# Attention plus a gated feed-forward block on one core: six of eight unrolled attention groups become a hardware loop, and four small VectorE instructions are written in plainer forms

## The chip, the cores and the metric

The kernel runs on one core of one Trainium2 chip. A core has five engines, each with a queue of its own: TensorE (PE; its weight loads are listed apart as PEld), VectorE (DVE), ScalarE (ACT), GpSimd (POOL) and SyncE (SP), which here only issues DMAs. "PEq", "DVEq" and so on are the queues' own instructions. Engines wait for each other by semaphores. The metric is the device time of one execution in microseconds (us). Before the change it is 1223.88 us, the median of 3 runs (1222.38 to 1224.13).

## The reference, cut to what matters

```python
# x: (2, 2048, 256), 16 heads of 16
xn = layernorm(x)
q, k, v = split(einsum('btd,ed->bte', xn, w_in), 3)        # per head
att = einsum('bhqd,bhkd->bhqk', q, k) / sqrt(16)
att = where(causal, att, 0.0)                              # masked scores are 0, not -inf
out = einsum('bhqk,bhkd->bhqd', softmax(att), v)
y_attn = einsum('btd,ed->bte', out, w_out)
x_prev = shift xn by one token
xr, xk = mu_r*xn + (1-mu_r)*x_prev, mu_k*xn + (1-mu_k)*x_prev
y_ffn = sigmoid(xr @ W_r.T) * (square(relu(xk @ W_k.T)) @ W_v.T)
return x + y_attn + y_ffn
```

Since a masked score is 0 and not minus infinity, keys behind the diagonal still take part, each with the weight exp(0 - max).

## The kernel before, in words

Stage 1 (`stage_tokens`) normalises the tokens in chunks of 512, computes q, k, v and the feed-forward part, and stores them in DRAM. q and k are each split into three bf16 parts. It already has a hardware loop over its first sequence, which runs once; all numbers in it are constants.

Stage 2 (`stage_attention`) works through eight groups, G = 2i + p: i runs over the two sequences and the two halves of the channels, p over two groups of four heads in each. p also says which of two sets of buffers the group uses. A group has four units u of 512 queries. Unit u has 4(u + 1) key tiles kt of 128 keys. For each key tile and each of 4 heads h:

- TensorE computes the scores (L1090) into a ring of 3 PSUM buffers, ScalarE takes the exponential (L972) into a ring of 16 SBUF buffers, and two tiles later TensorE multiplies with the values (L1104). On the diagonal GpSimd masks a 128x128 block first (L920); a `sem_inc` stands ahead of each mask (L918).
- Between them TensorE computes "pieces" of scores (L236) of a later unit or of the next group, of which VectorE takes the row maxima: L251 for a whole piece, L247 with a mask for one on the diagonal. Ahead of L247 stands a `sem_inc` (L246) that waits for the piece.
- Behind the last piece of a unit come six small VectorE instructions (`max_step`, k = 0 to 5), each on 128 partitions x 16 elements. They turn the maximum into a negative shift in three bf16 parts, which become three rows of the operand of L1090.

Once per unit TensorE adds the keys behind the diagonal (L1114), with diagonal weights that GpSimd makes with one product of 128x2048 (L887). ScalarE copies the sums out (L959), and VectorE divides them (L1007 to L1018). Once per group SyncE loads the next group's q, k (12 DMAs, L199 and L200) and v_sb (L219), after unit 0 has ended. GpSimd then adds up 15 tiles of v_sb one behind the other (L228), ahead of unit 2's masks, and TensorE and ScalarE make the suffix sums in unit 3. The last group also computes the output tiles (L1136).

What sets the order: each engine's instructions stand in its queue in the order of its `group` function, by the tables `SHIFT_AT`, `SV_AT`, `SLOT_PIECES`. The counts that the waits compare with grow from group to group, and are built from G, u and kt. Before the change G is a Python number everywhere, so every wait has a constant.

Of the kernel before, what the change touches and what calls it, by code (L numbers as in the profile page):

```python
# [7 lines left out]
ALU = mybir.AluOpType  # L8
# [4 lines left out]
B, T, C = 2, 2048, 256  # L13
# [3 lines left out]
CC = C // P  # L17
CH = 512
NCH = T // CH
SUB = CH // P  # L20
# [103 lines left out]
class Operands:  # L124
# [129 lines left out]
    def max_step(self, dve, k, u, n, reduced):  # L254


        by_head = [self.shift[:, u, :, part].rearrange("p s h -> p h s") for part in range(3)]
        if k == 0:
            dve.wait_ge(self.piece_reduced, reduced + MRING)
            dve.tensor_reduce(self.raw_max[:].rearrange("p h s -> p (h s)"), self.part_max[:, u % 2, :, 0:u + 1], AX_X,  # L260
                              ALU.max).then_inc(self.raw_ready, 1)
        if k == 1:
            dve.wait_ge(self.raw_ready, n + 1)
            dve.scalar_tensor_tensor(self.row_max[:, u], self.raw_max[:], 1.0, self.floor[:, :, u * SUB:(u + 1) * SUB],  # L264
                                     ALU.mult, ALU.max).then_inc(self.max_ready, 1)
        if k == 2:
            dve.wait_ge(self.max_ready, n + 1)
            dve.scalar_tensor_tensor(by_head[0], self.row_max[:, u], -1.0, self.floor[:, :, 0:SUB],
                                     ALU.mult, ALU.add).then_inc(self.hi_ready, 1)
        if k == 3:  # L270
            dve.wait_ge(self.hi_ready, n + 1)
            dve.scalar_tensor_tensor(self.shift_rest[:], self.row_max[:, u], -1.0, by_head[0], ALU.mult,
                                     ALU.subtract).then_inc(self.rest_ready, 1)
        if k == 4:
            dve.wait_ge(self.rest_ready, n + 1)
            dve.scalar_tensor_tensor(by_head[1], self.shift_rest[:], 1.0, self.floor[:, :, 0:SUB],
                                     ALU.mult, ALU.add).then_inc(self.mid_ready, 1)
        if k == 5:
            dve.wait_ge(self.mid_ready, n + 1)
            dve.scalar_tensor_tensor(by_head[2], self.shift_rest[:], 1.0, by_head[1], ALU.mult,  # L280
                                     ALU.subtract).then_inc(self.shift_ready, 1)

    def after_piece(self, dve, f, n0, base, close):

# [459 lines left out]
def stage_attention(nc, ops, ident, ident16, attn_t, ffn_d, w_out_sb, out):  # L744
# [7 lines left out]
    with ExitStack() as ctx:  # L752
# [56 lines left out]
        def unit_of(i, p, u):  # L809

            return (i * 2 + p) * NCH + u

        @block.sync
        def _(sp):
            def place_shift(p, u, n):

                sp.wait_ge(shift_t_ready, n + 1)
                for part in range(3):
                    sp.dma_start(q_op[ROWS + part:ROWS + part + 1, p, :, u * CH:(u + 1) * CH],
                                 shift_t[part * GH:(part + 1) * GH, u % 2]).then_inc(shift_loaded[u % 2], 16)  # L820

            def keep_normed(i, p, u):

                sp.wait_ge(normed_ready, unit_of(i, p, u) + 3)
                for h in range(GH):
                    row = (p * GH + h) * HD
                    sp.dma_start(attn_t[row:row + HD, i, u * CH:(u + 1) * CH],
                                 normed[h * HW:h * HW + HD, u % 2]).then_inc(normed_stored[u % 2], 16)

            def store_chunk(n):  # L830
                sp.wait_ge(total_ready, SUB * (n + 1))
                sp.dma_start(out_tiles[n], total[n % ORING]).then_inc(out_stored[n % ORING], 16)

            def group(i, p, first=False, last=False):
                if not first:
                    keep_normed(i - 1 + p, 1 - p, NCH - 1)
                place_shift(p, 2, unit_of(i, p, 2))
                if not last:

                    sp.wait_ge(out_ready, unit_of(i, p, 0) + 1)  # L840
                    ops.load_group(sp, i + p, 1 - p)
                keep_normed(i, p, 0)
                keep_normed(i, p, 1)
                place_shift(p, 3, unit_of(i, p, 3))
                if last:
                    store_chunk(0)
                keep_normed(i, p, 2)
                if not last:
                    place_shift(1 - p, 0, unit_of(i, p, NCH))
                    place_shift(1 - p, 1, unit_of(i, p, NCH + 1))  # L850
                if last:
                    for n in range(1, OUT_CHUNKS):
                        store_chunk(n)
                    keep_normed(i, p, NCH - 1)
                    for n in range(OUT_CHUNKS, B * NCH):
                        store_chunk(n)


            sp.sem_inc(probs_ready, SRING)
            sp.sem_inc(probs_used, USED)  # L860
            sp.sem_inc(out_ready, 1)
            sp.sem_inc(sums_ready, 1)
            sp.sem_inc(normed_ready, 2)
            for half in range(2):
                sp.sem_inc(normed_stored[half], STORES)
                sp.sem_inc(shift_loaded[half], SHIFTS)
            place_shift(0, 0, 0)
            place_shift(0, 1, 1)
            group(0, 0, first=True)
            for i in range(B * CC - 1):  # L870
                group(i, 1)
                group(i + 1, 0)
            group(B * CC - 1, 1, last=True)
            for s in normed_stored:
                sp.wait_ge(s, STORES * (1 + B * NG * NCH // 2))
            for s in out_stored:
                sp.wait_ge(s, 16 * (B * NCH // ORING))

        @block.gpsimd
        def _(pool):  # L880
# [16 lines left out]
            def group(i, p, first=False, last=False):  # L897
                G = i * 2 + p
                for u in range(NCH):
                    if u == 2 and not last:  # L900

                        pool.wait_ge(v_after_ready, G * 4 + 4)
                        ops.add_up_after(pool, 1 - p, G + 1, i + 1 + p)
                    if last and u == 1:
                        pool.wait_ge(out_ready, unit_of(i, p, 0) + 1)
                        for n in range(ORING):
                            load_chunk(n)
                    if last and u == NCH - 1:
                        for n in range(ORING, B * NCH - 1):
                            load_chunk(n)  # L910
                    if u == NCH - 1 and not last:
                        spread_weight(0, unit_of(i, p, NCH))
                    for kt in range(SUB * u, SUB * u + SUB):
                        for h in range(GH):

                            slot = (KT0[u] + kt) * GH + h
                            pool.wait_ge(probs_ready, G * SLOTS + slot + 1 + SRING)
                            pool.sem_inc(passed, 1)  # L918
                            blk = probs[:, slot % PRING, 0:P]
                            pool.affine_select(out=blk, in_=blk, compare_op=ALU.is_ge, fill=0.0, base=0,  # L920
                                               pattern=[[1, P]], channel_multiplier=-1).then_inc(probs_masked, 1)
                    if last and u == NCH - 1:
                        load_chunk(B * NCH - 1)
                    if u < NCH - 1:
                        spread_weight(u + 1, unit_of(i, p, u + 1))

            spread_weight(0, 0)
            group(0, 0, first=True)
            for i in range(B * CC - 1):
                group(i, 1)  # L930
                group(i + 1, 0)
            group(B * CC - 1, 1, last=True)
# [2 lines left out]
        def _(act):  # L935
# [53 lines left out]
            for u in range(2):  # L989
                weight(u, u)  # L990
            group(0, 0, first=True)
            for i in range(B * CC - 1):
                group(i, 1)
                group(i + 1, 0)
            group(B * CC - 1, 1, last=True)
# [2 lines left out]
        def _(dve):  # L998
# [49 lines left out]
                        add_tile(k)  # L1048

            group(0, 0, first=True)  # L1050
            for i in range(B * CC - 1):
                group(i, 1)
                group(i + 1, 0)
            group(B * CC - 1, 1, last=True)
# [2 lines left out]
        def _(pe):  # L1057
# [124 lines left out]
            for u in range(2):  # L1182
                turn_shift(u, u, 0)
            group(0, 0, first=True)
            for i in range(B * CC - 1):
                group(i, 1)
                group(i + 1, 0)
            group(B * CC - 1, 1, last=True)
# [28 lines left out]
```

## Time and profile before

| | |
|---|---|
| median of 3 runs | 1223.88 us (1222.38 to 1224.13) |
| the profiled execution | 1224.13 us, span 1222.3 us |
| PE busy | 1127.3 us (92%), 7168 matmuls |
| DVE busy | 949.4 us (78%) |
| ACT busy | 743.4 us (61%) |
| POOL busy | 347.7 us (28%) |
| stage 2 begins | about 242 us |
| groups 1 to 6 | 371 to 1094 us, 120 to 121 us each |

Busy time is the time in which an engine executes at least one instruction. The ends of matmuls are modelled and overlap, so TensorE's 92% is not TensorE at its peak. Register, branch, semaphore and DMA-issuing instructions are not counted as busy. The chain of waits is followed back from the last instruction, at each step to what released it; "issue" in it is time in which the engine waited for nothing that the profile shows.

### The profile page before, as it was taken

To read this page: it belongs to the slowest core of one execution; us is meant where nothing else is said; L and a number is where in the kernel's file an instruction comes from. 1 tells how busy PE (TensorE), PEld (TensorE's weight loads), DVE (VectorE), ACT (ScalarE), POOL (GpSimd) and SP (SyncE) were. 2 spreads that over 40 slices of the span, in tenths; PEclk is the share of its full clock that TensorE was granted. 3 is DMA by queue.
4 is the path that set the end of the run, shared out by engine and by line. 5 is a ranking of instruction groups with operands and counts; after the bars stand their busy time and mean duration, and the time that the engine had idled before them with its cause. 6 is when DMAs were issued, how large, how long until landed. Compare 5 with 4: busy or idle time off the path is not lost.

```text
span 1222.3 us, 21443 instructions
## 1 busy us (share of the span) xinstructions
PE 1127.3 (92%) x7168; PEld 459.4 (38%) x7168; DVE 949.4 (78%) x2433; ACT 743.4 (61%) x1553; POOL 347.7 (28%) x716
## 2 busy tenths in 40 slices
PE   5889888789999999999999999999999999999998
PEld 3656544343333333333333333333233332333345
DVE  5757888778689858986888788778968986899623
ACT  3544433166766666667667766766677666666773
POOL 2212113132423232334132323332332233224121
PEclk9999999889999989999999999999999999999999
DMA  4577732309001900180028002700360045002033
GB/s 129 164 185 172 213 109 91 104 3 144 9 2 23 130 6 2 24 129 6 2 32 122 6 1 39 114 6 2 53 100 6 1 60 94 6 1 79 6 108 108
DMA packets 62353, 79.22 MB, mean 65 GB/s; under 512 B 7075, under 2 KB 52515, under 8 KB 61219
## 3 DMA queue, kind: packets, MB, share of 16 engines
q1 hardware_dynamic: 61091, 73.66, 30.1%
q0 software_dynamic: 1152, 4.19, 1.2%
q8 instruction: 57, 0.93, 0.3%
q14 instruction: 53, 0.43, 0.1%
HBM read 43.78 MB, written 29.36 MB: 60 GB/s over the span
## 4 chain that ended last, share of the span: by engine, by line
PE 49%; DVE 12%; DMA 9%; issue 4%; SPq 2%; POOL 2%; ACT 1%; DVEq 0%; POOLq 0%
PE ps_o L1104 15%; PE ps_s L1090 14%; PE ps_m L236 13%; DMA v_sb<-vpad_d 9%; DVE part_max L251 5%; DVE ps_m L247 3%; PE ps_m L1136 2%; PE ps_o L1114 2%; POOL after L228 2%; DVE row_max L264 1%; PE ps_x L1081 1%; DVE part_max L247 1%; PE ps_x L1082 1%; DVE turned L1007 1%; SPq L200 1%
## 5 line engine op out<-in xcount | busy, mean ns | idle before, releaser
L972 ACT ACTIVATE probs<-ps_s 128x512 f32<-128x512 f32 (+3 forms) x1280 | 610.2, 534 | 290.0 <-PE ps_s L1090 285.1
L251 DVE TENSOR_REDUCE part_max<-ps_m 128x1 f32<-128x512 f32 x730 | 473.8, 680 | 33.7 <-PE ps_m L236 32.2
L1090 PE MATMUL ps_s<-q_op,k_op 99*128 99x512 bf16 (+3 forms) x1280 | 431.1, 355 | 8.8 <-ACT probs L972 6.0
L236 PE MATMUL ps_m<-k_op,q_op 96*128 96x512 bf16 (+3 forms) x1200 | 402.5, 355 | 33.5 <-DVE part_max L251 23.4
L247 DVE CUSTOM_DVE_ANT_0 ps_m<-ps_m,mask 128x384 f32<-128x384 f32 x470 | 229.2, 496 | 122.1 <-PE ps_m L236 120.4
L1104 PE MATMUL ps_o<-probs,v_sb 128*32 128x512 f32 (+3 forms) x2560 | 303.0, 546 | 4.8 <-POOL probs L920 4.8
L920 POOL TENSOR_SCALAR_AFFINE_SELECT probs<-probs 128x128 f32<-128x128 f32 x512 | 143.2, 296 | 396.3 <-ACT probs L972 389.6
L1090 PEld LDWEIGHTS ps_s<-q_op,k_op 99*128 99x128 bf16 x1280 | 122.0, 98 | 325.2 <-ACT probs L972 219.3
L236 PEld LDWEIGHTS ps_m<-k_op,q_op 96*128 96x128 bf16 x1200 | 117.9, 98 | 199.4 <-DVE part_max L251 92.6
L887 POOL TENSOR_TENSOR diag_weight<-ident,masked_weight 128x2048 f32<-128x2048 f32 x32 | 115.5, 3610 | 121.2 <-ACT masked_weight L939 121.2
L1104 PEld LDWEIGHTS ps_o<-probs,v_sb 128*32 128x32 f32 x2560 | 50.8, 108 | 94.0 <-issue 36.7
L228 POOL TENSOR_TENSOR after<-after,v_sb 128x64 f32<-128x64 f32 x120 | 40.0, 333 | 134.2 <-DMA v_sb<-vpad_d 125.4
L247 DVE DVE_READ_ACCUMULATOR2_ANT part_max<- 128x1 f32 x512 | 71.6, 140 | 0.0
L670 PE MATMUL ps_qk<-xn_t,w_in_sb 128*128 128x512 f32 x128 | 60.6, 609 | 1.7 <-ACT xn_t L597 1.4
L441 POOL TENSOR_TENSOR k_act<-k_act 128x1024 f32<-128x1024 f32 x8 | 15.4, 1919 | 126.5 <-ACT k_act L635 126.5
L602 ACT ACTIVATE parts<-ps_qk 128x512 bf16<-128x512 f32 x32 | 19.0, 594 | 46.7 <-PE ps_qk L670 46.7
L236 PE MATMUL ps_pieces<-k_op,q_op 96*128 96x512 bf16 (+2 forms) x80 | 25.6, 355 | 18.4 <-DVE part_max L251 9.2
L446 POOL TENSOR_TENSOR ffn<-ffn,x_in 128x512 f32<-128x512 f32 x16 | 21.5, 1342 | 57.8 <-DVE ffn L525 57.8
L607 ACT CAST parts<-rest 128x512 bf16<-128x512 f32 x32 | 19.7, 616 | 28.9 <-DVE rest L513 28.9
L1114 PE MATMUL ps_o<-diag_weight,v_after 128*32 128x128 f32 x1024 | 37.2, 291 | 0.0
L670 PEld LDWEIGHTS ps_qk<-xn_t,w_in_sb 128*128 128x128 f32 x128 | 24.4, 196 | 26.8 <-issue 22.5
L1136 PE MATMUL ps_m<-w_out_sb,attn_t 128*128 128x256 f32 x128 | 31.6, 381 | 0.5 <-DVE v_sb L1025 0.5
(84 smaller groups left out, 819.7 us busy)
## 6 DMA issues: line engine op xcount, KB each, us to landing
parts_d<-parts SPq DMA_DIRECT2D x48, 256.0 KB, 3.2
q_op<-parts_d SPq DMA_DIRECT2D x42, 256.0 KB, 13.1
k_op<-parts_d SPq DMA_DIRECT2D x42, 256.0 KB, 15.2
vpad_d<-v_pad SPq DMA_DIRECT2D x32, 256.0 KB, 3.5
v_sb<-vpad_d SPq DMA_DIRECT2D x8, 1024.0 KB, 26.8
x_in<-x SPq DMA_DIRECT2D x8, 512.0 KB, 5.4
ffn_d<-ffn SPq DMA_DIRECT2D x8, 512.0 KB, 3.2
attn_t<-normed SPq DMA_DIRECT2D x128, 32.0 KB, 2.0
```

The costliest lines, as they stand in the source:

```text
L228: pool.tensor_tensor(self.after[:, j], self.after[:, j + 1], values[:, j + 1, :, 0:HD], ALU.add).then_inc(self.after_ready, 1)
L236: last = pe.matmul(ps_m[:, f % ring, 0:width], self.q_op[0:ROWS, p, h, q0:q0 + P], self.k_op[0:ROWS, p, h, pc * CH:pc * CH + width], start ...
L247: dve.tensor_tensor_reduce(ps_m[:, f % ring, 0:width], ps_m[:, f % ring, 0:width], self.mask16[:, CH - width:CH], 1.0, LOWEST, ALU.add, AL ...
L251: dve.tensor_reduce(self.part_max[:, u % 2, h * SUB + s, pc:pc + 1], ps_m[:, f % ring, 0:width], AX_X, ALU.max).then_inc(self.piece_reduce ...
L670: last = pe.matmul(ps_qk[:, j % 2], w_in_sb[:, cc, j * P:(j + 1) * P], xn_t[:, cc, 1:CH + 1], start=(cc == 0), stop=(cc == CC - 1))
L887: pool.tensor_tensor(diag_weight[:, u % 2], ident[:].unsqueeze(1).broadcast_to([P, GH * SUB, P]), masked_weight[:, u].unsqueeze(2).broadca ...
L920: pool.affine_select(out=blk, in_=blk, compare_op=ALU.is_ge, fill=0.0, base=0, pattern=[[1, P]], channel_multiplier=-1).then_inc(probs_mas ...
L972: act.activation(probs[:, slot % PRING, 0:width], ps_s[:, slot % SRING, 0:width], ACT.Exp).then_inc(probs_ready, 1)
L1090: pe.matmul(ps_s[:, slot % SRING, 0:CH - q0], k_op[0:KROWS, p, h, kt * P:(kt + 1) * P], q_op[0:KROWS, p, h, u * CH + q0:(u + 1) * CH], sta ...
L1104: last = pe.matmul(ps_o[h * HW:(h + 1) * HW, q0:CH], v_sb[:, p, kt, h * HW:(h + 1) * HW], probs[:, ((KT0[u] + kt) * GH + h) % PRING, 0:CH ...
L1114: last = pe.matmul(ps_o[h * HW:(h + 1) * HW, s * P:(s + 1) * P], v_after[:, p, u * SUB + s, h * HW:(h + 1) * HW], diag_weight[:, u % 2, h ...
L1136: last = pe.matmul(ps_m[:, k % MRING, 0:C], attn_t[:, b * CC + cc, c * CH + t * P:c * CH + (t + 1) * P], w_out_sb[:, cc], start=(cc == 0), ...
```

## The change

In stage 2, the Python loop over groups 1 to 6 becomes `Fori`, a loop that each engine runs in its own queue: three rounds of two groups, `group(i, 1)` and `group(i + 1, 0)`. i is then a register. Group 0 and group 7 stay outside. The functions called are the same; a wait's number that depends on i is computed from the register before the wait, and so is the address of a DMA that depends on i. In `max_step`, four instructions that used a multiplication by one, or the zero constant `floor`, as a third operand are written without it.

```diff
         if k == 1:
             dve.wait_ge(self.raw_ready, n + 1)
-            dve.scalar_tensor_tensor(self.row_max[:, u], self.raw_max[:], 1.0, self.floor[:, :, u * SUB:(u + 1) * SUB],
-                                     ALU.mult, ALU.max).then_inc(self.max_ready, 1)
+            dve.tensor_tensor(self.row_max[:, u], self.raw_max[:], self.floor[:, :, u * SUB:(u + 1) * SUB],
+                              ALU.max).then_inc(self.max_ready, 1)
         if k == 2:
             dve.wait_ge(self.max_ready, n + 1)
-            dve.scalar_tensor_tensor(by_head[0], self.row_max[:, u], -1.0, self.floor[:, :, 0:SUB],
-                                     ALU.mult, ALU.add).then_inc(self.hi_ready, 1)
+            dve.tensor_scalar(by_head[0], self.row_max[:, u], -1.0, None, ALU.mult).then_inc(self.hi_ready, 1)
...
         if k == 4:
             dve.wait_ge(self.rest_ready, n + 1)
-            dve.scalar_tensor_tensor(by_head[1], self.shift_rest[:], 1.0, self.floor[:, :, 0:SUB],
-                                     ALU.mult, ALU.add).then_inc(self.mid_ready, 1)
+            dve.tensor_copy(by_head[1], self.shift_rest[:]).then_inc(self.mid_ready, 1)
         if k == 5:
             dve.wait_ge(self.mid_ready, n + 1)
-            dve.scalar_tensor_tensor(by_head[2], self.shift_rest[:], 1.0, by_head[1], ALU.mult,
-                                     ALU.subtract).then_inc(self.shift_ready, 1)
+            dve.tensor_tensor(by_head[2], self.shift_rest[:], by_head[1], ALU.subtract).then_inc(self.shift_ready, 1)
...
             place_shift(0, 0, 0)
             place_shift(0, 1, 1)
             group(0, 0, first=True)
-            for i in range(B * CC - 1):
+            with sp.Fori(0, B * CC - 1) as i:
                 group(i, 1)
                 group(i + 1, 0)
             group(B * CC - 1, 1, last=True)
... (the same for pool, act, dve and pe)
```

What stands in TensorE's queue, at the beginning of a unit 1: before,

```order
L1114 MATMUL ps_o<-diag_weight,v_after 32x128 [waits v_after_ready,diag_ready]
L1114 MATMUL ps_o<-diag_weight,v_after 32x128 x15
L1090 MATMUL ps_s<-q_op,k_op 128x512 [waits probs_ready]
L236 MATMUL ps_m<-k_op,q_op 128x256 [waits piece_reduced]
L1090 MATMUL ps_s<-q_op,k_op 128x512 [waits probs_ready]
L236 MATMUL ps_m<-k_op,q_op 128x512 [waits piece_reduced]
```

and in the loop (the lines of the new kernel are 3 lower; ISA is a register instruction):

```order
L1107 ISA
L1108 ISA [waits diag_ready]
L1111 MATMUL ps_o<-diag_weight,v_after 32x128 [waits v_after_ready]
L1111 MATMUL ps_o<-diag_weight,v_after 32x128 x15
L1086 ISA
L1087 MATMUL ps_s<-q_op,k_op 128x512 [waits probs_ready]
L234 ISA
L236 MATMUL ps_m<-k_op,q_op 128x256 [waits piece_reduced]
L1086 ISA
L1087 MATMUL ps_s<-q_op,k_op 128x512 [waits probs_ready]
L234 ISA
L236 MATMUL ps_m<-k_op,q_op 128x512 [waits piece_reduced]
```

The matmuls keep their order; ahead of each one that waits stands a register instruction. SyncE's queue, at the loads of the next group (the twelve loads alternate between q_op and k_op): before,

```order
L199 DMA q_op<-parts_d 16x4x2048 [waits out_ready]
L200 DMA k_op<-parts_d 16x4x2048
L199 DMA q_op<-parts_d 16x4x2048
L200 DMA k_op<-parts_d 16x4x2048
```

and in the loop:

```order
L837 ISA
L199 ISA [waits out_ready]
L199 DMA q_op<-parts_d 16x4x2048
L200 ISA
L200 DMA k_op<-parts_d 16x4x2048
L199 ISA
L199 DMA q_op<-parts_d 16x4x2048
L200 ISA
L200 DMA k_op<-parts_d 16x4x2048
```

Each load has a register instruction ahead of it, since its address depends on the round; one more stands ahead of v_sb (L219).

## Rows read from the trace of the kernel before

**Rows 1.** The page: span, and busy time, share and instructions of two engines.
```profile
span 1222.3 us, 21443 instructions
PE 1127.3 (92%) x7168; PEld 459.4 (38%) x7168; DVE 949.4 (78%) x2433; ACT 743.4 (61%) x1553; POOL 347.7 (28%) x716
```

**Rows 2.** Busy time of each engine in six stretches, groups 1 to 6.
```profile
core 0: us, PE busy (x) PEld busy (x) DVE busy (x) ACT busy (x) POOL busy (x), PEclk, DMA share, GB/s
371.00:491.00 120.00, 113.56 (x787) 38.87 (x785) 97.76 (x260) 79.22 (x174) 36.08 (x80) 0.97 0.28 41
...
852.00:973.00 121.00, 115.47 (x848) 40.62 (x846) 102.59 (x271) 82.71 (x180) 38.53 (x88) 1.00 0.27 41
...
sum 723.00, PE 686.87 PEld 237.63 DVE 598.73 ACT 485.55 POOL 222.04; mean PE 114.48 PEld 39.60 DVE 99.79 ACT 80.92 POOL 37.01
```

**Rows 3.** The chain of waits, 383 to 1104 us, shares by line.
```profile
by line: PE ps_o L1104 18.9%; PE ps_m L236 17.4%; PE ps_s L1090 17.2%; DMA v_sb<-vpad_d 11.4%; DVE part_max L251 6.8%; issue 5.5%; DVE ps_m L247 4.7%; PE ps_o L1114 2.9%; POOL after L228 2.0%; DVE part_max L247 1.3%; DVE turned L1007 1.2%; 
```

**Rows 4.** Who waited for whom, 383 to 1104 us: total us, times, longest.
```profile
PEld ps_s L1090 <- ACT probs L972: 164.0, 244, 0.8
PEld ps_m L236 <- DVE part_max L251: 75.1, 149, 1.9
PEld ps_o L1104 <- ACT sums L959: 4.5, 11, 0.4
```

**Rows 5.** The chain of waits, 634 to 641 us: start, us, what.
```profile
639.98 0.43 SPq L200
```

**Rows 6.** The chain of waits, 640 to 690 us.
```profile
640.45 26.99 DMA v_sb<-vpad_d
...
673.46 0.09 POOL probs L920
673.55 0.11 issue
673.67 0.02 POOLq L918
673.68 0.03 issue
...
674.55 1.06 PE ps_o L1104 x8
```

**Rows 7.** Instructions in order of time, 666 to 682 us, with idle time before.
```profile
673.46 2.76 POOL L920 TENSOR_SCALAR_AFFINE_SELECT probs<-probs 128x128 f32<-128x128 f32 x11
...
674.54 0.16 PEld L1104 LDWEIGHTS ps_o<-probs,v_sb 128*32 128x32 f32 x8 [0.91 <-POOL probs L920]
```

**Rows 8.** The chain of waits, 679 to 681 us.
```profile
680.08 0.02 DVEq L246
680.10 0.28 issue
```

**Rows 9.** Instructions in order of time on PEld, 866.9 to 868.5 us.
```profile
866.98 0.90 PEld L1114 LDWEIGHTS ps_o<-diag_weight,v_after 128*32 128x32 f32 x32
```

**Rows 10.** Instructions in order of time, 228 to 252 us.
```profile
242.07 0.33 PEld L1067 LDWEIGHTS ps_x<-ident,shift 128*12 128x12 bf16 x4 [1.60 <-issue]
```

**Rows 11.** The page's DMA queues: packets, MB, share of 16 engines.
```profile
q8 instruction: 57, 0.93, 0.3%
q14 instruction: 53, 0.43, 0.1%
```

**Rows 12.** Single lines of `max_step`: duration ns min/median/max, first and last start.
```profile
L264 DVE SCALAR_TENSOR_TENSOR row_max<-raw_max,floor x32: 150/171/2214, 158.3 to 1151.1; 128x16 f32<-128x16 f32 x32
L268 DVE SCALAR_TENSOR_TENSOR shift<-row_max,floor x32: 210/219/376, 159.2 to 1151.3; 128x16 bf16<-128x16 f32 x32
L276 DVE SCALAR_TENSOR_TENSOR shift<-shift_rest,floor x32: 212/222/371, 164.2 to 1151.8; 128x16 bf16<-128x16 f32 x32
```

**Rows 13.** Instructions in order of time, 618 to 632 us.
```profile
619.92 3.61 POOL L887 TENSOR_TENSOR diag_weight<-ident,masked_weight 128x2048 f32<-128x2048 f32 x1
...
621.94 1.62 DVE L264 SCALAR_TENSOR_TENSOR row_max<-raw_max,floor 128x16 f32<-128x16 f32 x1
```

More of the change, by code:

```diff
@@ L928, in _ @@
             group(0, 0, first=True)
-            for i in range(B * CC - 1):
+            with pool.Fori(0, B * CC - 1) as i:
                 group(i, 1)
@@ L991, in _ @@
             group(0, 0, first=True)
-            for i in range(B * CC - 1):
+            with act.Fori(0, B * CC - 1) as i:
                 group(i, 1)
@@ L1050, in _ @@
             group(0, 0, first=True)
-            for i in range(B * CC - 1):
+            with dve.Fori(0, B * CC - 1) as i:
                 group(i, 1)
@@ L1184, in _ @@
             group(0, 0, first=True)
-            for i in range(B * CC - 1):
+            with pe.Fori(0, B * CC - 1) as i:
                 group(i, 1)
```

## The prediction

> **What bounds the kernel now.** I read the table of busy shares first [rows 1]: TensorE is busy 1127.3 us of 1222.3, VectorE 949.4. The kernel is bound by TensorE, with VectorE close behind. The attention stage is eight groups (two sequences x four sets of four heads), and the change turns groups 1 to 6 into a loop of three rounds. The table of six stretches, cut where a group begins, is next [rows 2]: each group takes 120 to 121 us, TensorE is busy 686.87 of 723.00 us, VectorE 598.73. So whatever is added to TensorE's queue beyond what its work hides costs time at once, six times.
>
> The chain of waits for the same stretch [rows 3] says what runs out last. TensorE's three main lines hold 53.5%, the loads of v_sb with the sums on GpSimd behind them 13.4%, VectorE's piece reductions (L251, L247 and the accumulator read) 12.8%, and gaps in which no engine works ("issue") 5.5%. The table of waits [rows 4] adds that TensorE's weight loads sit idle 164.0 us for ScalarE's exponentials and 75.1 us for VectorE. Most of that idle time is weight loading waiting while a matmul still runs, so it is not free time of TensorE. Two places matter below. The first is at 640 to 675 us [rows 5, 6]: SyncE issues twelve loads and then v_sb at 0.43 us each, v_sb lands 26.99 us later, GpSimd adds up 15 tiles, then catches up with 11 masks that piled up meanwhile, and TensorE has been held for 0.91 us by them [rows 7]. The second is at 680 us [rows 8], where VectorE stands still 0.28 us behind its own sem_inc, because that one waits for the piece in the queue and nothing behind it has been prepared.
>
> **What the change adds: register arithmetic.** In the loop every semaphore target depends on the round, so the program has to compute it: the order shows a row "ISA" ahead of nearly every waiting instruction. I count them in the loop body of two groups: 808 on TensorE, 416 on VectorE (its other ISA rows are the masked reductions that were there before), 448 on ScalarE, 176 on GpSimd, 76 on SyncE. Per group that is 404, 208, 224, 88 and 38. Each is two to six operations on registers and does nothing on the engine itself.
>
> No row shows such an instruction. From below, a sem_inc, which only the queue handles, takes 0.02 us [rows 6, 8]. From above, the longest that a queue spends on one instruction here is 0.43 us for a DMA issue [rows 5]. I take 0.11 us: it is the gap between two masks of the backlog [rows 6], in which GpSimd's queue has to deal with one wait and one sem_inc. The whole forecast scales with this number, c.
>
> The Trainium skill, Advanced Engine Details and Errata, section Control Flow Timing, gives about 108 ns for a compare-and-branch; no row here shows one. If a register instruction cost the same, the sum below would stay where it is.
>
> *TensorE's own queue.* A group has about 800 pairs of weight load and matmul (787 to 848 matmuls in a stretch, [rows 2]). The queue can hand out 32 pairs in 0.90 us [rows 9], 0.028 us a pair, so 800 pairs need 22 us of queue time. 404 register instructions at 0.11 us add 44 us. Together 67 us of the 120.5, so the queue still runs ahead on average and this costs nothing, until c reaches (120.5 - 22) / 404 = 0.24 us. What is not hidden is a place where the queue itself has stood in a wait: diagonal weights, kept sums, a turned shift, a suffix sum and the head of a unit, 5 in each of 4 units, 120 in the six groups. There the next matmul starts later by one register instruction. For one of them, the kept sums, the trace shows 11 real waits in 24 units [rows 4], about half. 120 x 0.5 x 0.11 = 6.6 us. The bounds are 0 and 120 x 3 x 0.11 = 40 us.
>
> *VectorE.* Behind a plain reduction of 0.68 us the queue has time for a register instruction and the next one, which costs nothing. A masked reduction (L247) has the sem_inc ahead of it, so preparation begins only when the piece is there. L247 has 4.7% of the chain over 721 us [rows 3], 34 us, or 68 of them at 0.5 us. One register instruction each: 68 x 0.11 = 7.5 us. Bounds: 0 and, if all 384 of the loop were on the path, 42 us.
>
> *ScalarE.* An exponential takes 0.53 us on average, a register instruction and its own handling fit beneath it. Nothing is charged. The cover is gone only for the 128-wide ones if c passes about 0.2 us.
>
> *The path through v_sb.* Fourteen register instructions now stand on SyncE's queue between the release and the load of v_sb: 14 x 0.11 = 1.5 us. All thirteen loads share the DMA engines (4 MB in 32 us), so half of the delay reaches the landing, 0.8 us. GpSimd's additions are 0.33 us each and hide theirs. The backlog of 11 masks does not: it runs at 2.76 / 11 = 0.25 us each [rows 7] although the mask itself holds the chain for only 0.09 of it [rows 6], so it is the queue that sets the pace, and 11 x 0.11 = 1.2 us is added. 2.0 us in each of six groups, all of whose loads are issued inside the loop: 12 us. Bounds 0 and, with c = 0.43 and the whole delay landing, 6 x 10.7 = 64 us.
>
> **What it adds: the loop itself.** Each engine adds one to its counter and branches, and goes back twice. The nearest row is the jump from the first stage to the second: TensorE's weight loads stand 1.60 us [rows 10], a barrier included. 2 x 1.6 = 3.2 us; bounds 0 and 2 x 5 engines x 1.6 = 16 us if they stall one after another.
>
> The Trainium skill speaks against this part: Runtime: NRT & Kernel Launch, section Instruction fetch mechanics, says that instructions are prefetched in sequence only and that a taken branch to a page not held stalls until it is fetched. Rows agree with streaming: the two instruction queues move 1.36 MB in 110 packets [rows 11] for 21443 executed instructions, 64 bytes each, so nothing is reused. TensorE's body of about 4000 instructions is then 260 KB, fetched again in each round. A stall per return is what I charged above; by the rule alone it has no size.
>
> **What it replaces: four small VectorE instructions per unit.** The three-operand forms took 0.17, 0.22, 0.22 us in the median [rows 12]; their plain counterparts read one source less or skip a multiplication by one, on the same 16 elements per partition. 0 us. From below, 0.05 us less for each of four in 32 units is 6 us of VectorE, of which 13% on the chain, about 1 us gained. From above: L264 is the one that waits, 1.62 us beside GpSimd's 3.61 us product [rows 13], once a group; if the copy and the scaled write came to wait in the same way, 8 x 1.5 = 12 us. The new L264 has the same two inputs, so I leave its wait as it is.
> The Trainium skill, SBUF — State Buffer, section SBUF: two separate sides, says that a VectorE instruction with two SBUF inputs and a GpSimd one share a port pair that is locked for a whole instruction. By it L264 keeps its wait and the copies lose the reason for one; the trace agrees for L264.
>
> **The sum.** 6.6 + 7.5 + 12 + 3.2 + 0 = 29 us on the profiled execution's 1224.13 us (span 1222.3), which is 0.25 above the median of 1223.88. That gives 1253 us.
>
> **The rivals.**
> *Hidden.* All register work disappears in queues that run ahead, only the returns cost: 1224 + 3 = 1227 us. For it: TensorE's queue needs 67 of 120 us, TensorE hardly idles. Against it: the backlog of masks and VectorE's gaps are set by queues already [rows 6, 8].
> *The queue becomes the bound.* From c = 0.24 us on TensorE's queue needs more than a group lasts, and from 0.2 on in the stretches with narrow tiles. At 0.27 a group would be 22 + 404 x 0.27 = 131 us, 11 more, 66 in all, and the three other c-terms grow from 26 to 64: 1224 + 66 + 64 + 3 = 1357. At 0.2 only those terms grow, to 47, with some narrow stretches: about 1285. Middle 1320 us. For it: 0.43 us for a DMA issue shows that queues can be slow. Against it: 0.02 us for sem_inc.
> *Faster.* The plain L264 no longer waits for GpSimd. Its wait stands in the chain at the end of unit 2 of the maxima, about 1.5 us in each of eight groups: 1224 - 12 = 1212 us. It decides the sign only if the loop is free too, that is with c below some 0.03 us. Against it: two SBUF inputs remain.
>
> **Chances.** The forecast (1233 to 1290) 0.54, hidden (1224 to 1233) 0.22, queue as bound 0.19, faster 0.05. A measurement of this kernel can tell 0.2%, 2.4 us, from no change. Of the hidden case about 0.10 lies within that, and 0.01 below: faster 0.06, same 0.10, slower 0.84. The range 1226 to 1325 leaves out some 0.12 below and 0.07 above.
>
> **What would show it.** Six equal stretches of 124 to 125 us instead of 120.5, and groups 0 and 7 unchanged, show the per-group cost. The backlog of masks at 0.36 instead of 0.25 us each, and SyncE's loads at about 0.58 instead of 0.47 us apart, give c directly. TensorE's idle time would move from ScalarE to "issue" if its queue is the bound. If the pitch of the masks stays 0.25, or the span of a loop group stays 120.5, I am wrong toward "hidden"; if the weight loads wait for "issue" a hundred times a group, toward "bound". A gap on every engine at two moments a third of the loop apart shows the returns. L264 under 0.3 us everywhere would show the third rival.

## The result and the profile after: 1.2% slower, most of it at two moments

The changed kernel takes 1235.05 us, the median of 6 runs (1232.92 to 1243.44); beside it the kernel before took 1223.13 us (6 runs, 1216.68 to 1226.99). The ratio is 1.012, with a 95% interval of 1.0079 to 1.0162. The forecast was 1253 us, the range 1226 to 1325.

The profiled execution of the new kernel took 1247.56 us, 12.5 above the median of its kernel; the one of before took 1224.13, which is that kernel's usual time. So the two traces differ by 23 us where the kernels differ by 12. Part of what follows is the luck of that one execution, and is marked so.

The page of the new kernel, for [rows 1] and [rows 11]:

```profile
span 1245.8 us, 26838 instructions
PE 1140.9 (92%) x7168; PEld 472.1 (38%) x7168; DVE 950.6 (76%) x2433; ACT 743.8 (60%) x1553; POOL 347.6 (28%) x716
...
q8 instruction: 68, 1.11, 0.4%
q14 instruction: 86, 0.70, 0.2%
```

The matmuls are the same, 5395 more instructions run, and the instruction queues move 1.81 MB instead of 1.36. In the table of waits of the new kernel, 372 to 1094 us, this row has no partner in before (total us, times, longest):

```profile
PE ps_s L1087 <- issue: 8.1, 2, 4.1
```

Twice TensorE stands about 4 us with nothing that the profile shows to wait for. These are the loop's two returns, at the ends of groups 2 and 4. The new kernel in order of time, at the first of them:

```profile
611.07 0.60 PE L236 MATMUL ps_m<-k_op,q_op 96*128 96x512 bf16 x2
...
615.68 0.10 PEld L1087 LDWEIGHTS ps_s<-q_op,k_op 99*128 99x128 bf16 x1 [4.45 <-issue]
615.69 0.60 PE L1087 MATMUL ps_s<-q_op,k_op 99*128 99x512 bf16 x1 [4.02 <-issue]
...
616.33 0.60 ACT L969 ACTIVATE probs<-ps_s 128x512 f32<-128x512 f32 x1 [4.78 <-PE ps_s L1087]
...
616.80 0.57 DVE L247 CUSTOM_DVE_ANT_0 ps_m<-ps_m,mask 128x384 f32<-128x384 f32 x1 [4.03 <-PE ps_m L236]
```

ScalarE and VectorE wait for TensorE, TensorE for nothing. The first matmul behind the gap takes 0.60 us; this shape took 0.38 before. The stretches around it tell why (new kernel, columns as in [rows 2]; the granted clock is the third number from the end):

```profile
610.00:612.00 2.00, 1.67 (x14) 0.45 (x12) 1.99 (x5) 0.56 (x2) 0.73 (x3) 1.00 0.00 0
612.00:614.00 2.00, 0.00 (x0) 0.00 (x0) 0.77 (x2) 0.00 (x0) 0.00 (x1) 1.00 0.09 20
614.00:616.00 2.00, 0.31 (x1) 0.21 (x2) 0.00 (x0) 0.00 (x0) 0.00 (x0) 0.80 0.06 12
616.00:618.00 2.00, 2.00 (x6) 0.60 (x4) 0.66 (x3) 1.27 (x3) 0.46 (x2) 0.50 0.03 8
618.00:620.00 2.00, 2.00 (x11) 0.48 (x11) 1.25 (x2) 0.62 (x2) 0.42 (x2) 0.50 0.02 4
620.00:622.00 2.00, 2.00 (x7) 0.76 (x5) 1.47 (x4) 1.49 (x3) 0.59 (x2) 0.50 0.00 0
622.00:624.00 2.00, 2.00 (x46) 1.44 (x45) 0.84 (x4) 0.77 (x2) 0.59 (x2) 0.99 0.00 0
```

TensorE's granted clock falls from 2.4 to 1.2 GHz (1.00 to 0.50) while the engine stands, and stays there for some 6 us after. So a return costs twice: the gap, then work at half speed. The only traffic in the gap is 12 to 20 GB/s.

One number of the chain is a trap. For 383 to 1104 us it gives "issue" 20.7%, against 5.5% in [rows 3]. Four of its pieces are like this one (chain of the new kernel):

```profile
524.02 23.14 issue
```

They stand where before had 27 us of "DMA v_sb<-vpad_d" [rows 6]; every engine works meanwhile. Only the link from the load to its issue is missing, now that the address comes from a register.

A unit, measured from one block of masked keys (L1114, now L1111) to the next, shows both. Unit 3 takes 51.6 to 52.0 us in before; in the new kernel it takes 58.6 and 58.7 in groups 2 and 4 and 52 elsewhere. Groups 1 to 6 are 27.0 us longer in the new trace (what stands ahead of them was 3.6 us shorter there), and 13.7 of these are the units 3 of groups 2 and 4.

Most of the rest, 9.4 us, is in the units 2. A unit 2 takes about 31.6 us, or up to 37 where TensorE was held at its start by GpSimd's masks, behind v_sb:

| group | 1 | 2 | 3 | 4 | 5 | 6 |
|---|---|---|---|---|---|---|
| before: longest wait there, us | 1.65 | – | 0.91 | 1.17 | – | 1.35 |
| before: unit 2, us | 35.7 | 31.6 | 32.4 | 32.6 | 31.6 | 35.5 |
| after: longest wait there, us | 1.45 | 2.44 | 1.25 | 2.06 | 0.87 | 2.10 |
| after: unit 2, us | 35.6 | 36.6 | 32.8 | 36.3 | 32.7 | 34.8 |

The case of 2.44 us in the new kernel, in order of time, and the stretches behind it:

```profile
554.17 0.20 PEld L1101 LDWEIGHTS ps_o<-probs,v_sb 128*32 128x32 f32 x8 [2.44 <-POOL probs L917]
```

```profile
552.00:554.00 2.00, 0.00 (x0) 0.00 (x0) 0.00 (x0) 0.41 (x2) 1.83 (x7) 0.94 0.01 3
554.00:556.00 2.00, 1.83 (x8) 0.20 (x8) 0.00 (x0) 0.00 (x0) 1.84 (x8) 0.50 0.00 0
556.00:558.00 2.00, 1.74 (x16) 0.59 (x12) 0.00 (x0) 1.00 (x4) 0.98 (x4) 0.50 0.00 0
```

Again the engine stands, and the clock is halved for some 6 us. In the table the clock fell to 0.50 behind each wait of 1.35 us and more, and stayed at 1.00 behind those of 0.87 to 1.25 us. Length alone does not decide it: at another place, the end of unit 0, a wait of 1.41 us in before left the clock at 1.00 (505.84 us) and one of the same length was followed by 0.50 (983.58 us). Which of the two a group gets differs in both kernels. The experiments have to separate this scatter from the change.

### The profile page after: what moved, and what is told of

Its sections match the earlier page's. It is cut to its first block, busy times and chain, and to the rows that moved or that the text cites. A ratio compares the mean times of both kernels' runs of the same rounds, so it can differ in the third digit from the quotient of the medians.

```text
span 1245.8 us, 26838 instructions
## 1 busy us (share of the span) xinstructions
PE 1140.9 (92%) x7168; PEld 472.1 (38%) x7168; DVE 950.6 (76%) x2433; ACT 743.8 (60%) x1553; POOL 347.6 (28%) x716
## 4 chain that ended last, share of the span: by engine, by line
PE 54%; issue 13%; DVE 9%; POOL 2%; DVEq 1%; ACT 1%; POOLq 0%; DMA 0%; SPq 0%; ACTq 0%
PE ps_o L1101 17%; PE ps_s L1087 16%; PE ps_m L236 15%; DVE part_max L251 3%; PE ps_m L1133 2%; PE ps_o L1111 2%; DVE ps_m L247 2%; POOL after L228 1%; DVE row_max L264 1%; DVE part_max L247 1%; PE ps_x L1078 1%; PE ps_x L1079 1%; ACT probs L969 1%; DVE turned L1004 1%; PE ps_x L1064 1%
## 5 line engine op out<-in xcount | busy, mean ns | idle before, releaser
L251 DVE TENSOR_REDUCE part_max<-ps_m 128x1 f32<-128x512 f32 x730 | 474.6, 681 | 36.8 <-PE ps_m L236 35.1
L1087 PE MATMUL ps_s<-q_op,k_op 99*128 99x512 bf16 (+3 forms) x1280 | 437.3, 360 | 16.8 <-issue 8.1
L236 PE MATMUL ps_m<-k_op,q_op 96*128 96x512 bf16 (+3 forms) x1200 | 407.5, 359 | 34.0 <-DVE part_max L251 24.4
L1101 PE MATMUL ps_o<-probs,v_sb 128*32 128x512 f32 (+3 forms) x2560 | 307.2, 553 | 9.6 <-POOL probs L917 9.6
L236 PEld LDWEIGHTS ps_m<-k_op,q_op 96*128 96x128 bf16 x1200 | 118.7, 99 | 191.7 <-DVE part_max L251 85.7
L438 POOL TENSOR_TENSOR k_act<-k_act 128x1024 f32<-128x1024 f32 x8 | 15.3, 1918 | 123.0 <-ACT k_act L632 123.0
L443 POOL TENSOR_TENSOR ffn<-ffn,x_in 128x512 f32<-128x512 f32 x16 | 21.5, 1342 | 57.6 <-DVE ffn L522 57.6
L1111 PE MATMUL ps_o<-diag_weight,v_after 128*32 128x128 f32 x1024 | 37.5, 292 | 0.0
L667 PEld LDWEIGHTS ps_qk<-xn_t,w_in_sb 128*128 128x128 f32 x128 | 24.5, 196 | 27.1 <-issue 22.8
L1133 PE MATMUL ps_m<-w_out_sb,attn_t 128*128 128x256 f32 x128 | 31.6, 381 | 0.5 <-DVE v_sb L1022 0.5
```

What stands on the lines that cost most here:

```text
L236: last = pe.matmul(ps_m[:, f % ring, 0:width], self.q_op[0:ROWS, p, h, q0:q0 + P], self.k_op[0:ROWS, p, h, pc * CH:pc * CH + width], start ...
L251: dve.tensor_reduce(self.part_max[:, u % 2, h * SUB + s, pc:pc + 1], ps_m[:, f % ring, 0:width], AX_X, ALU.max).then_inc(self.piece_reduce ...
L667: last = pe.matmul(ps_qk[:, j % 2], w_in_sb[:, cc, j * P:(j + 1) * P], xn_t[:, cc, 1:CH + 1], start=(cc == 0), stop=(cc == CC - 1))
L1087: pe.matmul(ps_s[:, slot % SRING, 0:CH - q0], k_op[0:KROWS, p, h, kt * P:(kt + 1) * P], q_op[0:KROWS, p, h, u * CH + q0:(u + 1) * CH], sta ...
L1101: last = pe.matmul(ps_o[h * HW:(h + 1) * HW, q0:CH], v_sb[:, p, kt, h * HW:(h + 1) * HW], probs[:, ((KT0[u] + kt) * GH + h) % PRING, 0:CH ...
L1111: last = pe.matmul(ps_o[h * HW:(h + 1) * HW, s * P:(s + 1) * P], v_after[:, p, u * SUB + s, h * HW:(h + 1) * HW], diag_weight[:, u % 2, h ...
```

## The experiments

Theories after the result. *Return*: the loop costs its two returns, each a stand for instructions and a stretch at half clock, and nothing else. *Arithmetic*: the register instructions cost too. *Scatter*: unit 2 varies by itself, up to some 10 us a run. Each experiment ran side by side with the kernel before, whose medians were 1226.14 us beside e1 to e4, 1229.50 beside e5 to e8, 1225.73 beside e9 to e11 and 1225.85 beside e12. So a time below is best read by its ratio. Where an edit is shown for TensorE (`pe`), the same was done on the engines that the text names.

**e1, the four VectorE forms alone.** All groups written out.

> Only the four VectorE instructions in plain form, groups 1 to 6 unrolled. If the loop is the whole cost, this is the kernel before: 1223 us, within 2.4. If the plain forms cost anything (a wait for GpSimd as L264 has), up to 8 x 1.5 = 12 us more; if they gain, about 1 us less.

1225.43 us, ratio 0.9991 (0.9967 to 1.0014). The forms cost and give nothing that can be measured. In the profiled execution, the slowest of its twelve at 1234.47 us, five of six units 2 took 34.8 to 36.8 us with no register instruction in the kernel: that is scatter.

**e2, the loop on TensorE alone**, old VectorE forms.

```diff
-            for i in range(B * CC - 1):
+            with pe.Fori(0, B * CC - 1) as i:
```

> Only TensorE loops over groups 1 to 6; the other four queues are unrolled with constants, and the old VectorE forms stand. Theory R (the returns of TensorE are the cost: 4.0 us of standing each and then 6 us at half the clock): nearly the whole difference, +10 to +13 us, so 1233 to 1236. Theory A (register arithmetic on the waits of all engines and on the path through v_sb is the cost): well under half, +2 to +5 us.

1237.40 us, ratio 1.0086 (1.0055 to 1.0118); units 3 of groups 2 and 4 took 57.6 and 57.7 us. One engine's loop costs about as much as five.

**e3, the loop on all engines with its first instructions asked for ahead of the return.**

```diff
-            with pe.Fori(0, B * CC - 1) as i:
+            with pe.bass.Fori(0, B * CC - 1, engines=OrderedEngineSet([pe.engine]), hint_back_edge=True) as i:
```

> The changed kernel, with a prefetch hint for the branch back at the top of each round on every engine, nothing else. If the 4 us at a return are the wait for instructions to be fetched (theory R with this cause), they go, TensorE does not lose its clock there, and the time comes back to 1223 to 1227 us. If a taken branch costs this by itself, or the arithmetic is the cost, it stays at 1233 to 1237.

1226.79 us, ratio 1.0007 (0.9982 to 1.0032), units 3 at the returns 52.4 and 52.3 us. The arithmetic and the branches are the same, the instructions at the target are asked for earlier, and the stand is gone: it was the wait for these instructions. At the same return TensorE is idle 0.55 us instead of 4.02, and the next matmul runs at full speed (e3, in order of time):

```profile
603.35 0.60 PE L237 MATMUL ps_m<-k_op,q_op 96*128 96x512 bf16 x2
...
604.50 0.39 PE L1088 MATMUL ps_s<-q_op,k_op 99*128 99x512 bf16 x1 [0.55 <-issue]
```

**e4, the arithmetic without the loop.** All groups written out on all five engines, but every number computed from a register that holds zero.

```diff
-            for i in range(B * CC - 1):
+            nought = pe.alloc_register("nought")
+            pe.reg_mov(nought, 0)
+            for k in range(B * CC - 1):
+                i = k + pe.snap(nought, min_val=-(k == 2), max_val=k < 2)
```

> No loop: groups 1 to 6 unrolled, but i is a constant plus a register that holds zero, on all five engines, so the same 5000 or so register instructions are executed as in the changed kernel, and no branch. Theory R: 1223 to 1227 us. Theory A: 1233 to 1237 us, the whole difference.

1235.40 us, ratio 1.0057 (1.0018 to 1.0097). Units 3 took 51.9 to 52.5. There are no returns, yet there are stands in the middle of groups. The chain of waits of e4:

```profile
652.64 0.61 ACT probs L975
653.25 3.27 issue
656.52 0.39 PE ps_s L1099
```

This run speaks for both Arithmetic and Scatter; e10 takes it up again.

**e5, one return instead of two.** The first round written out on every engine.

```diff
-            with pe.Fori(0, B * CC - 1) as i:
+            group(0, 1)
+            group(1, 0)
+            with pe.Fori(1, B * CC - 1) as i:
```

> The changed kernel with its first round written out on all engines and a loop over the other two rounds: one return instead of two, and the register arithmetic in four groups instead of six. Theory R with 5.8 to 6.7 us a return: half the difference, 5 to 7 us above before. Theory A: two thirds of it, 7 to 8 us; the profile decides between them: one unit 3 of 58 us instead of two.

1243.74 us, ratio 1.0106 (1.0068 to 1.0144): not half the cost, a miss for Return as it stood. The one return is there (854.76), with unit 3 of group 4 at 57.8 us. But the chain of e5 has three more stands where the loop does not go back, in the units 2 of groups 4, 5 and 6, and these units take 37.5, 38.1 and 36.9 us. TensorE's next matmul waits for nothing that the profile shows in each:

```profile
774.25 2.84 issue
...
854.76 3.81 issue
...
901.27 0.15 DVE part_max L247
901.42 3.69 issue
905.12 0.60 PE ps_m L236
...
1030.94 2.46 issue
```

The first and the last lie 5.2 us behind the start of their unit 2, groups 4 and 6: the same place of the loop's body, in both of its rounds. So *Return* is not the whole account: stands also come in the middle of a loop's body, and no run shows why they come here and not in the changed kernel.

**e6, the loop on all engines but TensorE**, the mirror of e2's edit, old VectorE forms.

> The mirror of the TensorE-only loop: the four other queues loop, TensorE is unrolled with constants, the old VectorE forms stand. If TensorE's return alone costs, because the others stand beside it, this is 1223 to 1228 us. If every engine's fetch is long enough to starve TensorE by itself, it is 8 to 13 us above before, and the two mirror kernels together cost more than the change.

1245.19 us, ratio 1.0134 (1.0094 to 1.0173). TensorE goes straight on and soon waits for the others, in the chain of e6 for VectorE's return:

```profile
610.21 0.68 DVE part_max L251
610.89 2.12 issue
...
613.91 1.42 issue
```

Units 3 at the returns took 56.4 and 56.0 us and the unit behind them 1 to 2 us more. So e2 and e6 together exceed the whole change. The units say the same without the scatter of units 2: at a return TensorE alone loses 5.7 and 6.1 us (e2), the four others lose 5.5 to 6.5 with the unit behind (e6), and all five together 6.6 and 7.0 (the changed kernel). When all engines go back at once, their stands overlap.

**e7, a short loop.** The kernel before, with this at the ends of groups 2 and 4 on TensorE.

```diff
+                if i < 2:
+                    with pe.Fori(0, 2):
+                        pe.sem_inc(again, 1)
```

> The kernel before, and on TensorE, where groups 2 and 4 end, a loop of two rounds that holds one increment of a semaphore that nobody waits for: two taken branches at the places of the two returns, but to an instruction that has just been executed. If the price of a return is that of fetching what lies at its target: nothing, within 2.4 us of before. If a taken branch or a compare stops TensorE's queue by itself: +8 to +13 us.

1231.22 us, ratio 1.0012 (0.9979 to 1.0044), units 3 there 52.5 and 52.2 us, 0.6 more than in before. TensorE stands 0.74 and 0.70 us there, and its clock stays up. In the median this is too little to be seen. So such a loop, with its counter and its branches, costs about 0.6 us; the rest of the 4 us comes with the distance of the jump.

**e8, v_sb first.** To take the scatter away, the kernel before with the load of v_sb ahead of the twelve q, k loads.

```diff
     def load_group(self, sp, i, p):
+        self.load_values(sp, i, p)
         for r in range(len(Q_PARTS)):
...
-        self.load_values(sp, i, p)
```

> The kernel before, with v_sb loaded ahead of the twelve loads of q and k instead of behind them. GpSimd's sums then start about 17 us earlier and are done when unit 2's masks come; TensorE is not held in unit 2, and its clock is not halved there. By the units 2 of the kernel before (32.5 to 35.7 us in three groups, 31.6 in the two without a long wait) 6 to 12 us below before, with less spread from run to run. If the q and k loads, 8 us later, hold up unit 3, it gains less or loses.

1212.79 us, ratio 0.9876 (0.9837 to 0.9915): below both kernels. GpSimd's sums now begin at 643.40 us, against 667.58 in before; no masks pile up, every unit 2 takes 31.6 to 31.8 us, and groups 1 to 6 last 118.1 to 120.1 us.

On this base the change was taken apart once more.

**e9, the changed kernel with v_sb first**, and **e12, the same without the loop** (all groups written out, plain forms).

> The changed kernel with v_sb loaded ahead of the twelve q and k loads, which in the unrolled kernel took away the wait for v_sb and with it the scatter of unit 2 (31.6 to 31.8 us in all groups, median 1212.8). Theory (the change costs its two returns, about 6.5 us each, and next to nothing besides): 1212.8 + 13 = 1226, units 3 of groups 2 and 4 at 58 to 59 us, all other units as in the unrolled kernel with the moved load. Rival (register arithmetic costs as well, about 7 us over six groups, as the run with arithmetic and no loop suggests): 1233.

> All groups written out, constants everywhere, the four plain VectorE forms, v_sb loaded first: the kernel with the loop and v_sb first (1226.72) without its loop alone. Theory (loop costs 12 to 13 us, the forms nothing, the moved load gains 13): 1213 us, ratio to the kernel before 0.988, units 2 of 31.6 to 31.8 us, units 3 of 51.6 to 51.9. Rival (the moved load's gain was luck of one call): 1220 to 1226, units 2 of 33 to 37 us in some groups.

e9: 1226.72 us (1223.25 to 1230.85), ratio 1.0009 (0.9978 to 1.0040). e12: 1213.12 us (1211.65 to 1216.80), ratio 0.9901 (0.9872 to 0.9930). The loop alone costs 13.6 us by the medians, or 1.1% by the ratios. The traces say where, in us by group:

| group | 1 | 2 | 3 | 4 | 5 | 6 |
|---|---|---|---|---|---|---|
| e12, no loop | 119.6 | 118.5 | 119.7 | 119.8 | 119.7 | 119.4 |
| e9, loop | 119.8 | 124.6 | 120.3 | 125.8 | 120.0 | 120.0 |

Groups 2 and 4, which end with a return, are 12.1 us longer together, the four others 1.7 us. Single groups of e8 and e12, which differ only in the forms, are up to 1.6 us apart, so 0.4 us a group is within what scatters. It agrees with the units 3 without a return, 52.0 us in e9 against 51.6 to 51.7. In e12 unit 3 of group 2 runs from one block of masked keys to the next like this (in order of time):

```profile
557.70 1.06 PE L1111 MATMUL ps_o<-diag_weight,v_after 128*32 128x128 f32 x32
...
609.62 1.06 PE L1111 MATMUL ps_o<-diag_weight,v_after 128*32 128x128 f32 x32
```

and in e9, with the return between them:

```profile
554.96 1.06 PE L1111 MATMUL ps_o<-diag_weight,v_after 128*32 128x128 f32 x32
...
606.79 0.60 PE L1087 MATMUL ps_s<-q_op,k_op 99*128 99x512 bf16 x1 [3.96 <-issue]
...
613.11 1.06 PE L1111 MATMUL ps_o<-diag_weight,v_after 128*32 128x128 f32 x32
```

58.15 instead of 51.92 us, 6.2 more: 3.96 of it is the stand, the rest the half clock (e9, stretches):

```profile
604.00:606.00 2.00, 0.00 (x0) 0.00 (x0) 0.00 (x0) 0.00 (x0) 0.00 (x0) 0.90 0.01 4
606.00:608.00 2.00, 1.21 (x4) 0.57 (x5) 0.10 (x1) 0.57 (x1) 0.00 (x0) 0.50 0.08 20
608.00:610.00 2.00, 2.00 (x12) 0.44 (x10) 1.23 (x4) 1.22 (x3) 0.80 (x3) 0.50 0.00 0
```

**e10, arithmetic without the loop, v_sb first.**

> Groups 1 to 6 written out, every number computed from a register that holds zero, plain VectorE forms, v_sb loaded first. No branch. Theory (arithmetic is hidden; the 7 us of the run without the moved load were the scatter of unit 2): 1213 to 1214. Rival A (arithmetic costs about 1 us a group on the engines' queues): 1220, with units evenly longer. Rival B (instructions that arrive late: the stray gaps of 2.5 to 3.7 us marked issue in the middle of groups, which no unrolled kernel without arithmetic has): 1216 to 1222, with one to three such gaps and single long units.

1228.86 us, ratio 1.0023 (0.9997 to 1.0050), 16 us above e12. The time lies above all three forecasts; of the mechanisms, Rival B's stands are there. Groups 1 and 2 take 120.0 and 118.6 us, as if there were no arithmetic; from group 3 on single units 2 take 33.3 to 36.9. The chain of e10 has four stands of over 1 us in groups 3 to 6:

```profile
644.89 3.00 issue
...
741.46 1.41 issue
...
772.51 2.44 issue
...
1024.88 1.22 issue
```

The chain of e4 has four too (beside a piece of 23 us with the missing link), and three of them lie within 0.03 us of the same distance behind the last block of masked keys (the fourth within 0.2). They come back in two kernels at the same places of the program, so they belong to the instruction stream. In e9 the chain has no "issue" of over 1 us but at the two returns, and in e12 none at all, while e5, a loop, has three in mid-group. So neither "written out" nor "arithmetic" alone makes them. Why some streams have such stands stays open; that their instructions arrive late is a guess. It also bounds what e9 says: the arithmetic is nearly free in that loop, not in every program that holds it.

**e11, the loop with the hint, v_sb first.**

> The loop on all engines with its first instructions prefetched at the return, v_sb loaded first. Theory: the return is free and arithmetic hidden, 1213 to 1215, units 3 of groups 2 and 4 at 52 us. Rival (arithmetic or late instructions cost 7 us): 1220.

1220.17 us, ratio 0.9951 (0.9922 to 0.9980). Groups 1 to 5 take 118.7 to 120.7 us with units 3 of 52.0 to 52.4, so the returns cost no more than the 0.6 us of e7 each. By the medians the hint gives back 6.6 of the loop's 13.6 us; the program still ends 5 to 7 us later than e8 and e12. One piece shows in its chain at the end of group 6, just behind the place where the loop is left. e9, without the hint, has none there, so it comes with the hint; that the hint asked for the wrong instructions there is a guess:

```profile
1085.51 1.30 issue
```

Unit 3 of group 6 takes 53.8 us, group 7 112.0 against 110.4 to 110.7, and 2.4 us more lie behind the issue of the last store, when all engines have finished. e3 has the same two pieces, a stand of 1.56 us with a unit 3 of 55.2 us and the late end, so its 1.0007 does not show that a hinted loop is free. What causes the late end was not tried.

## Why the prediction was wrong

The direction was right and the range held the time. The forecast of 1253 was 18 us too high: it expected 29 us more, where the medians lie 12 us apart and the ratio of 1.012 makes some 15. Two errors of opposite sign lie in it, and that they partly cancel is luck: with my arithmetic and the measured returns I would have said 1262.

**The step that failed: register arithmetic at 6.6 + 7.5 + 12 = 26 us.** It measured 1.7 us in four groups of e9 against e12, 0.4 a group, about 2.6 in six. Its terms:

- *c itself.* I took 0.11 us. The new trace has rows for such instructions (ns min/median/max), 0.055 us on TensorE's queue and 0.069 on VectorE's, and the chain shows 0.06 to 0.09. The same sum with 0.069 would still give 16 us. So the size of c is the smaller part of the error; that these instructions hold anything up is the larger.

```profile
L1086 PEldq FUSED_REGOPS  x960: 55/55/60, 364.3 to 1113.5; - x192
L243 DVEq FUSED_REGOPS  x957: 69/69/86, 365.6 to 1114.8; - x192
...
606.12 0.08 DVEq L243
```

- *The backlog of masks, 11 x 0.11 us.* It runs as before, 11 masks in 2.76 us (new kernel, in order of time; compare [rows 7]). The pitch of 0.25 us was not a queue with no room left, as I had read [rows 6]; a register instruction fits in it.

```profile
677.69 5.93 POOL L228 TENSOR_TENSOR after<-after,v_sb 128x64 f32<-128x64 f32 x15 [18.56 <-DMA v_sb<-vpad_d]
683.57 2.76 POOL L917 TENSOR_SCALAR_AFFINE_SELECT probs<-probs 128x128 f32<-128x128 f32 x11
```

- *SyncE's fourteen instructions.* The loads stand 0.52 us apart, not 0.58, because the DMA issue itself became shorter than in [rows 5], and sums begin 26.2 us after v_sb is issued (27.1 before):

```profile
646.84 0.32 SPq L200 DMA_DIRECT2D k_op<-parts_d  x1
647.36 0.32 SPq L199 DMA_DIRECT2D q_op<-parts_d  x1
...
651.48 0.35 SPq L219 DMA_DIRECT2D v_sb<-vpad_d  x1
```

- *TensorE's exposed instructions, 6.6 us, and VectorE's, 7.5 us.* In the waits of 372 to 1094 us "PEld ps_s <- issue" holds 25.3 us in e12 and 33.9 in e9; less two returns of up to 4.4 us each that is the same number; the two smaller rows with "issue" grew by 3.4 us. TensorE's weight loads did not wait longer for VectorE either: "PEld ps_m <- DVE part_max" (both lines) is 120.8 us in e12 and 107.3 in e9. I charged half of TensorE's candidate places as exposed, and each masked reduction of VectorE's on the chain; the queues have slack at nearly all of them.

**The term that was mis-sized the other way: the returns.** I took 1.6 us each from the jump between the stages [rows 10], 3.2 in all. Two measured 12.1 us (e9 against e12, with the arithmetic of these two groups in it) and 13.7 (trace of the new kernel against before). The upper bound of 16 us held them, but by the wrong sum: it stacked five engines' stands, and these overlap (e2, e6). What I missed is that the stand is 4 us, not 1.6, and that 4 idle microseconds halve TensorE's clock afterwards. Of the Trainium skill's rule in Runtime: NRT & Kernel Launch, section Instruction fetch mechanics, that a taken branch to a page not held stalls until it is fetched, the runs agree: TensorE stands 4.02 us at the return over the long body and 0.74 us where the target has just been executed (e7). The section gives no size for the stall; here it is the 4 us.

**The rivals.** *Hidden* (1227) had the arithmetic right and shared my price of a return; with the measured price it would have said 1236, against 1235.05. *The queue becomes the bound*: no sign of it; c stayed below 0.1 us in every row. *Faster*: L264 kept its wait for GpSimd's product, as assumed (new kernel; compare [rows 13]):

```profile
631.65 1.60 DVE L264 TENSOR_TENSOR row_max<-raw_max,floor 128x16 f32<-128x16 f32 x1
```

**The plainer forms at 0 us**: right. They are a little shorter (medians 195 against 219 and 222 ns, [rows 12]), and e1 shows no gain. The longest copy took 0.35 us, so none waited out GpSimd's product of 3.61 us.

**The announced signs.** "Six equal stretches of 124 to 125 us" did not come: the new kernel has four of 121.2 to 123.0 us and two of 131.2 and 131.4, four of 120 and two of 124.6 and 125.8 are in e9. The pitch of the masks stayed at 0.25, which the prediction had named as being wrong toward "hidden". The gap on every engine at two moments came.

**The baseline.** I treated the 0.91 us of [rows 7] as a fixed cost of the path through v_sb. It was one draw of a wait that is longer in other groups and then costs 4 to 5 us by the clock. I also took the groups as 120 to 121 us each, from evenly cut stretches; from one block of masked keys to the next they take 118.2 to 123.6 us in before. Loading v_sb first gains 13 us in the unrolled kernel (e12: ratio 0.9901) or 17 (e8: 0.9876), at least as much as the loop costs. The best kernel here is e8, and e12 equals it within the runs' spread.

## What to carry to other kernels

Price a hardware loop by its returns first: with a long body each return stopped TensorE for some 4 us here, and the stretch at half clock behind it cost half as much again. A prefetch at the return removed both, but gave back only half of the loop's cost in all (e11). Register arithmetic ahead of waits was nearly free in the loop, where queues run ahead; look in the trace for stands in mid-group before trusting this (e4, e5, e10). When the time scatters by 1%, look for a wait of one to two microseconds on TensorE that sometimes halves the clock, and remove it before measuring a change of that size.

## What the runs showed of the hardware

- A register instruction ahead of a wait takes 0.055 us on TensorE's queue and 0.069 us on VectorE's.
- A load whose address comes from a register is mostly issued in 0.32 to 0.35 us on SyncE, one with a constant address in 0.41 to 0.45, in the same kernel too. The instructions ahead of it make up for that: the loads stand 0.52 us apart, against 0.47.
- A return over a body of about 4000 TensorE instructions: a stand of 3.4 to 4.1 us (e2, e5, e9, the changed kernel). With the prefetch: 0.51 to 0.55 us (e3, e11). A return over one instruction: 0.70 to 0.74 us (e7).
- Waits of 1.35 to 2.44 us ahead of unit 2 were followed by 3.4 to 6.8 us at half of TensorE's clock, as the 4 us stand was; those of 0.87 to 1.25 us were not (table above). At the end of unit 0 waits of 1.41 us were followed by either.
